# Keys of a cross-attention built with channels on partitions, their context pieces loaded into the place of the low parts, and a ring of five key heads

## The reference

```python
x = layernorm(x + self_attention(x))           # 16 heads of 32, causal
x = layernorm(x + cross_attention(x, ctx))     # 16 query heads of 128, 4 key/value heads, 361 context rows
x = layernorm(x + mixture_of_experts(x))       # 8 experts, 2 per token
# in the cross-attention
q = rmsnorm(x @ Wq + bq) * qn_w                # per head of 128 channels
k = rmsnorm(ctx @ Wk + bk) * kn_w              # 4 heads of 128 channels
v = ctx @ Wv + bv
out = softmax(q @ k.T / sqrt(128) + mask) @ v
```

## Time and profile before

| what | value |
|---|---|
| runs | 1504.46, 1507.34, 1509.42 us, median 1507.34 |
| profiled execution, its own time | 1511.84 us |
| its span, first to last instruction | 1510.0 us |
| mean granted TensorE clock | 0.977 of full speed |
| busy share | PE 93%, DVE 57%, ACT 47%, POOL 41% |
| queries' and keys' phase | self-attention to 436 us, cross-attention 436 to about 1289 us |

### The profile page before, as it was taken

One profiled execution on the slowest core, in us unless ns is written; L12 is line 12 of the kernel. 1 busy time (PEld: TensorE's weight loads), 2 busy tenths in 40 slices (PEclk: granted clock), 3 DMA queues, 4 the chain that ended last, 5 costly groups with the idle time before them and its releaser, 6 DMA issues. The chain is left out here.

```text
span 1510.0 us, 24824 instructions
## 1 busy us (share of the span) xinstructions
PE 1404.4 (93%) x8553; PEld 1180.6 (78%) x8553; DVE 862.4 (57%) x3010; ACT 715.8 (47%) x1885; POOL 612.9 (41%) x936
## 2 busy tenths in 40 slices
PE   7889999999987999999999999999999997499976
PEld 7678988887866788888888888888888886377854
DVE  2644353434346676667666766676667665743357
ACT  3655555556335444445444544444444445343246
POOL 1221211212116455455545554555455436344164
PEclk9999999999999999999999999999999999599998
DMA  6211111212434221222122212212221221675363
GB/s 197 90 34 45 66 60 63 77 34 67 141 124 119 58 66 37 64 59 57 46 64 59 58 46 64 56 48 58 58 58 37 73 66 68 229 214 161 107 220 106
DMA packets 70548, 126.57 MB, mean 84 GB/s; under 512 B 11835, under 2 KB 47007, under 8 KB 69528
## 3 DMA queue, kind: packets, MB, share of 16 engines
q1 hardware_dynamic: 65848, 110.04, 23.9%
q0 software_dynamic: 4576, 14.95, 3.5%
HBM read 93.50 MB, written 31.45 MB: 83 GB/s over the span
## 5 line engine op out<-in xcount | busy, mean ns | idle before, releaser
L1341 POOL TENSOR_TENSOR b_pcarry<-b_half 128x1 f32<-128x1 f32 x173 | 49.2, 284 | 370.7 <-DVE b_rinv L1204 347.4
L75 PE MATMUL bank<-b_kTh,b_q 128*100 128x362 f32 x512 | 171.4, 336 | 8.2 <-POOL b_q L1362 6.1
L1085 ACT ACTIVATE b_probs<-b_probs,b_nmax 100x361 f32<-100x361 f32 x256 | 152.0, 594 | 18.9 <-DVE b_nmax L1198 18.6
L1198 DVE CUSTOM_DVE_ANT_0 b_probs<-bank,b_mask 100x361 f32<-100x361 f32 x256 | 135.3, 529 | 44.5 <-issue 40.0
L1373 POOL TENSOR_SCALAR b_probs<-b_probs,b_rinv 100x361 f32<-100x361 f32 x256 | 148.2, 590 | 0.0
L1080 ACT ACTIVATE b_pTh<-bank 121x400 fp32r<-121x400 f32 x192 | 96.8, 505 | 101.7 <-PE bank L917 96.9
L1191 DVE TENSOR_TENSOR b_pTl<-bank,b_pTh 121x400 fp32r<-121x400 f32 x192 | 109.6, 571 | 56.9 <-ACT b_pTh L1080 56.9
L1133 ACT ACTIVATE b_oTh<-bank,b_bv 128x400 fp32r<-128x400 f32 x64 | 38.1, 595 | 211.3 <-PE bank L75 211.3
L431 ACT ACTIVATE a_probs<-a_probs,a_nmax 100x100 f32<-100x100 f32 x256 | 93.2, 367 | 46.8 <-DVE a_nmax L551 46.7
L917 PE MATMUL bank<-ident,b_probs 100*121 100x100 f32 x768 | 110.6, 266 | 4.4 <-POOL b_probs L1373 3.5
L917 PEld LDWEIGHTS bank<-ident,b_probs 100*121 100x121 f32 x768 | 108.2, 187 | 6.6 <-POOL b_probs L1373 4.4
(11 more groups left out here) (255 smaller groups left out, 3871.0 us busy)
## 6 DMA issues: line engine op xcount, KB each, us to landing
q_d<-a_qb SPq DMA_DIRECT2D x64, 200.0 KB, 2.3
b_q_raw<-q_d SPq DMA_DIRECT2D x64, 200.0 KB, 2.4
b_q_raw<-rs_d SPq DMA_DIRECT2D x64, 200.0 KB, 3.4
b_ctxr<-in_ctxT SPq DMA_DIRECT2D x48, 242.0 KB, 4.8
y_d<-c_y SPq DMA_DIRECT2D x32, 256.0 KB
c_Eraw<-in_expert_w SPq DMA_DIRECT2D x10, 512.0 KB, 6.8
a_stage<-in_Wq SPq DMA_DIRECT2D x4, 1024.0 KB
stage<-in_Wo SPq DMA_DIRECT2D x8, 512.0 KB, 4.6
```

What stands on the lines that cost most here:

```text
L75: mm = eng.matmul(out, lhsT=l(c), rhs=r(c), start=first and k == 0, stop=last and k == n - 1)
L1085: act.activation(p, p, ACT.Exp, scale=-1.0, bias=nmax[:, s % 2, h:h + 1], accum_out=psums[:, s % 2, h:h + 1]).then_inc(e_rdy, 1)
L1198: dve.tensor_tensor_reduce(out=probs[:, s % 2, h, 0:SE], in0=s_bank[h % 2][0:S, 0:SE], in1=mask_s[:], scale=-1.0, scalar=BIG, op0=ALU.add, ...
L1341: pool.tensor_tensor(pcarry[:, k:k + 1], half_s[:, 0:1], half_s[:, 0:1], ALU.add)
```

## The change

Keys after: PE computes one key head at a time with its 128 channels on partitions and all 362 context rows in the columns, so there is nothing to transpose. Everything else of the key path follows from that layout.

- `keys(j + 1, kv)` for kv = 0 to 3 has 12 matmuls of 362 columns. Head 0 stands at the end of step 1 and now waits for all three context pieces' low parts; heads 1 and 2 are the quarters of step 2, head 3 follows them.
- DVE adds the bias from PSUM (`key_bias`), ACT squares (`key_square`), PE sums over channels with a matmul against ones at the end of step 2 (`key_sums`). At the start of step 3 ACT makes exp(-0.5 ln) and its square (`key_root`), DVE corrects the root in two instructions (`key_newton`), SP stores the four rows to DRAM, waits, and loads them back spread over 128 partitions (`spread_key_roots`). DVE multiplies (`key_scale`), ACT and DVE write the parts. In step 3 `key_scale(j + 1, 0)` stands between `queries` and `masked(j, 3, 3)`, `keys_hi(j + 1, 0)` before `exponent(j, 3, 3)`. Heads 2 and 3 are finished in steps 0 and 1 of batch j + 1.
- Each context piece is loaded into the place of its own low part, and only when `values(j, c)` has read it. ACT writes the high part in step 1 (`context_hi`, after each of the first three exponents), POOL the low part over the raw one.
- Key parts lie in a ring of five heads; squares and unscaled keys use the same places before.
- The query roots get the same correction (`newton`, and one more ACT instruction in `roots`); their square sums go to another PSUM bank and later in PE's order.

The core of the diff (before is `-`, after is `+`):

```diff
 PE, cross-attention
-            def keys(jn, c, chunks=range(DC)):
-                    pe.wait_ge(ctx_lo, 3 * jn + c + 1)
-                mm = product3(pe, key_bank(jn, c)[0:KT, :], lambda i: ctxh[:, c, i, :], ...
-            def transpose_keys(jn, c): ...
+            def keys(jn, kv, chunks=range(DC)):
+                if chunks[0] == 0:
+                    if kv == 0:
+                        pe.wait_ge(ctx_lo, 3 * (jn + 1))
+                        pe.wait_ge(v_lo, 3 * jn)
+                    if kv >= 2:
+                        pe.wait_ge(k_sq_set, 4 * jn + kv - 1)
+                cols = slice(kv * XHD, (kv + 1) * XHD)
+                mm = product3(pe, key_bank(jn, kv)[:, 0:SEQ], lambda i: Wkh[:, i, cols], lambda i: Wkl[:, i, cols],
+                              lambda i: ctxh[:, i, 0:SEQ], lambda i: ctxl[:, i, 0:SEQ], ...
+            def key_sums(jn):
+                pe.wait_ge(k_sq_set, XKV * (jn + 1))
+                for kv in range(XKV):
+                    mm = pe.matmul(kv_bank[0][kv * SHD:(kv + 1) * SHD, 0:SEQ], lhsT=ones_s[:], rhs=k_sq[:, ...], start=True, stop=True)
@@ step 2 and 3
-                            keys(j + 1, 1, (q,))
+                            keys(j + 1, 1 + q // 2, range(2 * (q % 2), 2 * (q % 2) + 2))
+                            keys(j + 1, 3)
-                            transpose_keys(j + 1, 0)
-                            keys(j + 1, 2)
+                    if s == 2 and not last:
+                        key_sums(j + 1)
-                            transpose_keys(j + 1, 1)
-                            transpose_keys(j + 1, 2)
 SP
+                sp.wait_ge(v_done, KC * (jn - 1) + c + 1)
+                sp.dma_start(ctxr[:, :, c * KT:(c + 1) * KT], ctxT[KC * jn + c]).then_inc(ctx_in[c], 16)
+            def spread_key_roots(jn):
+                sp.wait_ge(k_rs, jn + 1)
+                for kv in range(XKV):
+                    sp.dma_start(kr_d[jn, kv].unsqueeze(0), krs[kv * SHD:kv * SHD + 1, :]).then_inc(krs_out, 16)
+                sp.wait_ge(krs_out, 16 * XKV * (jn + 1))
+                wait(sp, k_rdy, XKV * jn)
+                for kv in range(XKV):
+                    sp.dma_start(krb[:, kv], kr_d[jn, kv].partition_broadcast(P)).then_inc(k_in[kv], 16)
 ACT
+            def key_root(jn):
+                act.wait_ge(k_ss, jn + 1)
+                act.activation(krs[:], kv_bank[0][:, 0:SEQ], ACT.Ln, bias=rms_eps_s[:, 0:1]).then_inc(k_ln, 1)
+                act.activation(krs[:], krs[:], ACT.Exp, scale=-0.5).then_inc(k_root, 1)
+                act.activation(k_sq[:, XKV * jn % KS, 0:SEQ], krs[:], ACT.Square).then_inc(k_rt, 1)
+                    if s == 3 and not last:
+                        key_root(j + 1)
                     for h in range(3):
                         if before:
                             probs_hi(n - 1, h)
                         if now:
                             exponent(j, s, h)
+                        if s == 1 and not last:
+                            context_hi(j + 1, h)
                     if now:
                         queries_hi(n + 1)
+                        if s == 3 and not last:
+                            keys_hi(j + 1, 0)
                         exponent(j, s, 3)
 DVE
                         if before:
                             probs_lo(n - 1, h)
+                        if s == 3 and h == 0 and not last:
+                            key_newton(j + 1)
                     if now:
                         queries(n + 1)
+                        if s == 3 and not last:
+                            key_scale(j + 1, 0)
                         masked(j, s, 3)
                         invert_sums(j, s, 0)
+                        if s == 3 and not last:
+                            keys_lo(j + 1, 0)
+            def key_scale(jn, kv):
+                dve.wait_ge(k_in[kv], 16 * (jn + 1))
+                k_ = k_raw[:, (XKV * jn + kv) % KS, 0:SEQ]
+                dve.tensor_tensor(k_, k_, krb[:, kv], ALU.mult).then_inc(k_rdy, 1)
+                    if s < 2 and now:
+                        key_scale(j, s + 2)
+                        keys_lo(j, s + 2)
 POOL
-                    if not last:
-                        split_ctx(j + 1, 0)
-                        split_ctx(j + 1, 1)
+                        for c in range(KC):
+                            context_lo(j + 1, c)
```

More of the change, by code:

```diff
@@ L404, in _ @@
             square_sums(NQ // XG - 1)
-            context_keys(1)
-            context_keys(2)
+            for kv in range(1, XKV):
+                context_keys(kv)
         @block.scalar
@@ L501, in _ @@
                 head_squares(m[2])
-                if m[0] is not None:
-                    roots(m[0] // XG)
                 if i < GB and par == 1:
@@ L512, in _ @@
                 head_squares(m[3])
+                if m[0] is not None:
+                    roots(m[0] // XG)
             t = TAIL
@@ L656, in _ @@
                 queries(m[3])
+                if m[0] is not None:
+                    newton(m[0] // XG)
             t = TAIL
@@ L862, in body @@
                     if not last:
[L863 to L864 removed]
+                        for c in range(KC):
+                            load_ctx(j + 1, c)
                     load_q(4 * j + 2, 0, 16 * j + 4)
@@ L1129, in body @@
                             split_hi(KV_PIECES + 2 * s + k)
+                    if s == 1 and not last:
+                        key_square(j + 1, 0)
+                    if s == 2 and not last:
+                        key_square(j + 1, 2)
+                        key_square(j + 1, 3)
                     if before:
@@ L1140, in body @@
                             values_hi(j, c)
-                    if s in (2, 3) and not last:
-                        keys_hi(j + 1, s - 2, 1 - par)
+                    if s < 2 and now:
+                        keys_hi(j, s + 2)
                     if s == 3 and not last:
-                        keys_hi(j + 1, 2, 1 - par)
+                        keys_hi(j + 1, 1)
                 if past:
@@ L1257, in body @@
                         residual_norm(j - 1)
-                    if s in (1, 2) and not last:
-                        key_squares(j + 1, s - 1)
+                    if s == 1 and not last:
+                        key_bias(j + 1, 0)
                     if s == 2 and not last:
-                        key_squares(j + 1, 2)
+                        key_bias(j + 1, 2)
+                        key_bias(j + 1, 3)
                     if s == 3 and not first:
                         apply_norm(j - 1)
+                    if s < 2 and now:
+                        key_scale(j, s + 2)
                     if s == 3 and not last:
-                        key_norm(j + 1, 2)
+                        key_scale(j + 1, 1)
                     if before:
@@ L1281, in body @@
                     early = [equal_s[:], above_s[:]]
-                    late = [kn[0:S, 0, k * E * E:(k + 1) * E * E] for k in range(2)]
+                    late = [krb[0:S, XKV - 1, k * E * E:(k + 1) * E * E] for k in range(2)]
                     compare(early, 0, B - 1)
@@ L1373, in normalise @@
                     pool.tensor_scalar(p, p, rinv[:, s % 2, h:h + 1], 1.0, ALU.mult, ALU.mult).then_inc(p_rdy, 1)
-            pool.wait_ge(set_up, 4)
+            pool.wait_ge(set_up, 5)
             queries_lo(0)
-            for c in range(KC):
-                key_rsqrt(0, c)
             def body(j, par):
@@ L1384, in body @@
                     if not last:
-                        split_ctx(j + 1, 0)
-                        split_ctx(j + 1, 1)
+                        for c in range(KC):
+                            context_lo(j + 1, c)
                     normalise(j, 1)
-                    if not last:
-                        key_rsqrt(j + 1, 0)
-                        split_ctx(j + 1, 2)
                     normalise(j, 2)
@@ L1394, in body @@
                         expert_lo(1)
-                    if not last:
-                        key_rsqrt(j + 1, 1)
                 if not first:
@@ L1402, in body @@
                 if not past:
-                    if not last:
-                        key_rsqrt(j + 1, 2)
                     normalise(j, 3)
```

299 lines of the change are left out of this document (143 added, 156 removed).

## The result

The kernel after takes 1614.52 us (median of 4 runs, 1613.11 to 1617.58), the one before 1505.90 in the same comparison (1503.48 to 1509.42): a ratio of 1.072, 95% interval 1.069 to 1.075. It is slower by 108.6 us; 1608 was forecast.

The account below looks back on a forecast made before the run. PE was taken as the bound; gate 1.4, trip 4.3 and clock 1.5 gave 7.2 us per batch, 101 for 14 batches, plus 3 for batch 0. On 1507 that made 1611, put as 1608, range 1540 to 1650.

Parts of the forecast that it names:

- the gain on PE: PE's work falls 0.95 us per batch and 1.1 us of waiting goes; alone 30 us over 15 batches.
- The gate: Step 1, before keys(j + 1, 0): PE waits 2.2 us for the third context piece; step 1 grows by 1.4.
- Step 2 even: Step 2 keeps its length: three heads and the square sums replace two pieces and transposes with their waits.
- The trip: Step 3: key roots' way through DRAM delays masked(j, 3, 3); next batch's first transposes come 4.3 us later.
- The clock: Batch boundary: a lowered granted clock behind PE's new wait adds 1.5 us per batch, bounds 0 and 3.
- Rival (b): Context pieces in 484-byte rows land late, about 9.9 us into step 1: 1660 us; chance 0.12, shared with a second slow clock.
- (a): Rival: trip shorter or not slowing the clock, queues overlapping better; 1.4 + 1.4 per batch, 1550 us; chance 0.20.
- (c): Rival: the trip at the batch boundary is hidden and only PE's gain counts, 1477 us; chance 0.09.
- (d): Rival: trip hidden, step 1's 33 us of waits cancel PE's 30 us gain, 1510 us; chance 0.04.
- Costed at nothing: Query roots' correction in the self-attention phase taken as covered, else 8 us; removed work and ring also free.
- The start of the phase: Cross-attention start: roots' first trip beside values(0, 0..2) replaces the 3.46 us wait and slow clock: even.
- The sum: 7.2 us per batch for 14 batches, 101, plus 3 for batch 0: +104 us, 1611 for the median.

Follow-up runs that it names:

- e2g: Kernel after with two full context buffers: piece loads wait for no product of the previous batch, high and low copies made earlier; 1591.83 us.
- e1: Kernel after with key head 0's key_scale, keys_lo and keys_hi moved behind masked(j, 3, 3) and exponent(j, 3, 3), trip kept; 1543.81 us.
- e3: Kernel after without the key roots' DRAM trip for all batches but the first, queue places kept, output different; 1560.42 us.
- e7: Kernel after with the four rows of key roots stored and awaited twice, lengthening the trip; 1652.08 us.
- e5: Kernel after with 16 unused matmuls of 128 columns behind step 3's output product, keeping PE busy in its wait; 1588.74 us.
- e4: Kernel after with the query roots' correction removed and their square sums back in the old bank and place; 1605.71 us.
- e6b: Kernel after with the last two Wo pieces loaded ahead of the second trip of the roots, in batch 0; 1615.20 us.

## Why the prediction was right, point by point

The mechanism was the one forecast: the gain on PE is small, and the loop pays for a wait at the batch boundary, for the clock behind it and for a gate in step 1. The sizes came out near partly by luck, since errors of both signs cancel.

- **The gate, right.** 1.72 us of wait for 2.2 forecast, step 1 +1.2 for +1.4; e2g removes it. The forecast's chain is the one in the trace: third exponent, copy, low part. It came out smaller because the third exponent ends 5.9 us into the step and not 6.3, and PE comes at 6.2 and not 5.97. The load set nothing here.
- **Step 2 even, right:** 12.55 and 12.50.
- **The trip, right in mechanism, 1.3 us too long.** Root and newton end at 3.9 us into step 3 (forecast 4.15), the loads are issued at 5.9 (7.05), k_in comes at 9.05 (10.3). The mis-sized term is the stores: four take 1.11 us to issue and the last is down 0.9 us after, 2.0 in place of 2.9; I had scaled them from the query roots, where four took 2.37 and 0.97. Another 0.3 are the roots, 0.1 the load. masked(j, 3, 3) at 9.5 for 10.8, the transposes at 15.07 for 16.0: +3.35 for +4.3. e1, e3 and e7 show that the step is the cause.
- **The clock, right, too small:** 2.1 to 2.2 us for 1.5. e5 separates it.
- **Rival (b), late pieces, refuted.** It had the third piece 9.9 us into step 1; it lands 3.3 us into it, 2.6 us before ACT takes it. The median of all these loads is 3.1 us in after, where it was 4.8 before. That is not a gain from the narrow rows. Page of the profile, DMA issues, after and then e2g, which has the same rows of 484 bytes:

```profile
b_ctx_raw<-in_ctxT SPq DMA_DIRECT2D x48, 242.0 KB, 3.1
```
```profile
b_ctx_raw<-in_ctxT SPq DMA_DIRECT2D x48, 242.0 KB, 5.3
```

  The two kernels differ in when the loads are issued: in after one by one, some us apart, in e2g three together behind those of the queries. Like for like, by tile, "DMA to landing" is 2.6 us for a load issued alone before (at 877.39, rows of 1936 bytes) and 3.2 for one in after (at 880.92, rows of 484 bytes); issued together it is 5.0 to 5.1 for two before (from 862.94) and 4.9 to 6.2 for three in e2g (from 858.7). So the narrow rows cost about 0.5 us when alone, and the company of other loads about 2. The Trainium skill (DMA: Bandwidth & Descriptors, Specifications) gives 512 bytes as the least for line rate. The traces agree in sign, but the doubling that rival (b) took as its condition, a factor of my own, isn't there; packets under 512 bytes rise from 11835 to 37632.
- **Rivals (a), (c) and (d)** needed a trip that is hidden or slows nothing. e7's one-to-one answer excludes slack, and e3 shows for (a) that even without a trip the boundary is later than before.
- **Costed at nothing, wrong twice.** The query roots cost 9.2 us by the trace (e4). The start of the phase was not even: from the last query sums to the first statistics it is +7.1, where I had +3. PE's waits there grow from 17.1 to 25.6 us, with one of 8.0 on Wo's low part: the trip of batch 1 holds the last Wo pieces behind it on SP, a queue I hadn't walked in batch 0. In e3, where that trip is not made, the wait is 2.5 us and the stretch 107.1; in e6b it is 3.9 us and the stretch 108.6, where after has 108.9. A shorter wait gave back 1.8 and 0.3 us of the stretch, so the cause of the larger part of the 7.1 stays open.
- **The sum.** The loop costs 96.3 us where 101 stood: per batch trip -1.0, clock +0.7, gate -0.2. The start and batch 0 cost 17.0 where 3 stood. In all 113 for 104, with errors of both signs in it: the terms called even or free were 14 us too low, the loop 5 too high. The sum itself gave 1611 for the median; putting 1608 was no rounding of it and went the wrong way. Taking the runs' median and not the profiled execution as the base was right: that execution had the one-off stall of 9.4 us. By medians the difference is 108.6, by the traces 112.3; runs of either kernel spread over 4 to 6 us.

## What to carry to other kernels

An in-order engine that waits for a long round trip should have nothing behind it that another engine needs soon: moving key_scale and what follows it behind masked(j, 3, 3) was worth more here (68.7 us) than removing the trip and leaving them in place (52.1). When a layout removes work from the bounding engine but lengthens the chain between batches, look for work of the next batch that can stand in front of the chain's end, here one value piece. A product that comes to need several pieces at once waits for the last copy in another engine's queue: two buffers and an earlier place for the copies gave 20 us here, together. Before blaming a load, compare when it lands with when it is taken. An idle stretch of PE costs more than its length, by more than half here (3.6 and 2.1 us), so it is worth measuring with matmuls that compute nothing before the chain itself is taken apart.

## What was not expected of the hardware

- A wait of PE of 3.6 us was followed by 5.5 us at a granted clock of 0.50 (925.56 to 931.08), 2.1 us lost behind the transposes, in every batch; the wait of 1.72 us in step 1 was followed by none (1.00 in the first two windows of after).
- Shorter waits did and didn't lower the clock. In e3 PE waits 1.0 and 0.8 us at every batch boundary and 1.7 in every step 1. Behind the boundary at 681.27 the clock stays at 1.00; behind the one at 842.46 it is 0.50 from 844.46 on, with the same waits. Of its 14 full batches four have such a stretch behind the boundary and two behind the wait in step 1 (924.83 and 1034.33). e1 has one, behind its wait in step 1 at 761.02, and that is its one batch of 54.3 us where the others take 52.6. Windows of e3 from the two boundaries on:

```profile
681.27:683.27 2.00, 1.20 (x8) 0.89 (x8) 0.74 (x3) 0.00 (x0) 1.48 (x3) 1.00 0.84 240
683.27:685.27 2.00, 2.00 (x17) 1.77 (x17) 0.93 (x5) 1.08 (x3) 0.00 (x0) 1.00 0.12 29
...
842.46:844.46 2.00, 1.21 (x8) 0.89 (x8) 0.69 (x3) 0.00 (x0) 1.47 (x3) 0.99 0.89 243
844.46:846.46 2.00, 2.00 (x10) 1.52 (x9) 0.75 (x3) 1.08 (x3) 0.00 (x0) 0.50 0.14 33
```

- How many loads are issued together mattered far more than the width of their rows: the same 242 KB in rows of 484 bytes had a median of 3.1 us in after, where they are issued apart, and 5.3 in e2g, where three are issued together.
- From the first of four stores of 1448-byte rows to the end of the load of one of them, spread over 128 partitions, it was 5.2 us (915.89 to about 921.1), of which the issues of SP are 1.5.
